# AdaLN block on one core: waits for scores placed per bank, x and statistics of the second half moved by one step, loads of rows and experts spread over steps

## What is computed

```python
mod = silu(c) @ wmod                       # six rows of 512 per batch: sa, ca, ga, sb, cb, gb
h = layernorm(x) * (1 + ca) + sa
q = rope(h @ Wq.T)                         # 32 heads of 128
k = low-rank c_kv = h @ Wdk.T, with 64 rotated columns per KV head from h @ Wkr.T   # 8 KV heads
v = c_kv @ Wupv.T
x = x + ga * (causal_softmax(q @ k.T / sqrt(128)) @ v) @ Wo.T
h = layernorm(x) * (1 + cb) + sb
p = softmax(h @ router.T + bias)           # 64 experts
w = p where it is among the 8 largest of its row, else 0
x = x + gb * (h * w.sum() + w @ expert_bias)
```

## Time and profile before

| | us |
|---|---|
| three timed executions | 1570.37, 1567.42, 1570.78; median 1570.37 |
| the profiled execution | 1571.39, of which the span of instructions 1570.1 |
| PE busy | 1507.3 (96% of the span) |
| DVE, POOL, ACT busy | 1174.6 (75%), 1031.4 (66%), 971.1 (62%) |
| share of PE in the chain of work that ended last | 89% |

### The profile page before, as it was taken

How to read it: one execution, slowest core, us unless ns; L and a number is a source line. 1 busy time by engine, 2 the same in 40 slices (tenths; PEclk the granted TensorE clock), 3 DMA queues, 4 the chain that set the end, 5 groups by cost and what they waited for, 6 DMA issues and landing times.

```text
span 1570.1 us, 24850 instructions
## 1 busy us (share of the span) xinstructions
PE 1507.3 (96%) x7502; PEld 1268.7 (81%) x7502; DVE 1174.6 (75%) x3437; ACT 971.1 (62%) x2301; POOL 1031.4 (66%) x778
## 2 busy tenths in 40 slices
PE   8979999999999999999999999998999999999978
PEld 5668888888888888888888888887887778787865
DVE  6856777777777777777777787775888888977746
ACT  3356766676676666676767677664656555565651
POOL 1776767676676677667667667665767777765612
PEclk9989999999999999999999999999999999999987
DMA  8547665566556656656556656658688776767631
GB/s 310 203 165 215 192 213 185 187 208 207 181 198 206 197 190 204 201 196 214 179 191 215 201 173 210 204 184 228 207 241 269 226 244 212 249 219 245 219 90 47
DMA packets 208245, 319.00 MB, mean 203 GB/s; under 512 B 37153, under 2 KB 125985, under 8 KB 208113
## 3 DMA queue, kind: packets, MB, share of 16 engines
q1 hardware_dynamic: 207792, 317.31, 62.9%
q10 hardware_dynamic: 320, 0.11, 0.0%
HBM read 177.71 MB, written 139.62 MB: 202 GB/s over the span
## 4 chain that ended last, share of the span: by engine, by line
PE 89%; DVE 3%; issue 3%; DMA 2%; ACT 1%; SPq 1%; POOL 1%; ACTq 0%; DVEq 0%
PE bank_s L465 22%; PE bank_o L563 21%; PE bank_pv L549 15%; PE bank_s L508 15%; PE bank_s L488 5%; PE bank_s L476 5%; PE bank_s L444 1%; PE bank_s L607 1%; PE bank_s L595 1%; DMA wmod<-in_wmod 1%; PE bank_o L412 1%; SPq L1639 1%; DMA PT_raw<-blocks 1%; DVE y L1037 1%; DMA blocks<-blocks 0%
## 5 line engine op out<-in xcount | busy, mean ns | idle before, releaser
L1460 POOL TENSOR_TENSOR PT_lo<-PT_raw,PT_hi 128x640 fp32r<-128x640 f32 x250 | 391.7, 1589 | 84.9 <-ACT PT_hi L841 84.8
L825 ACT ACTIVATE probs<-probs,row_inv 128x512 f32<-128x512 f32 x508 | 256.9, 554 | 169.7 <-DVE row_inv L1109 168.8
L1449 POOL TENSOR_TENSOR rot_c<-rot_c,rot_s 128x512 f32<-128x512 f32 x128 | 165.4, 1292 | 221.9 <-DVE rot_s L1070 221.9
L818 ACT ACTIVATE probs<-probs,row_min 128x512 f32<-128x512 f32 x508 | 278.4, 551 | 16.4 <-DVE row_min L1103 16.2
L1103 DVE CUSTOM_DVE_ANT_0 probs<-bank_s,mask 128x512 f32<-128x512 f32 x508 | 229.5, 487 | 0.9 <-issue 0.6
L1454 POOL TENSOR_TENSOR qT_lo<-rot_c,qT_hi 128x512 fp32r<-128x512 f32 x128 | 167.2, 1306 | 92.8 <-ACT qT_hi L800 92.8
L465 PE MATMUL bank_s<-hT_lo,wq_hi 128*128 128x512 f32 x500 | 205.2, 410 | 11.4 <-issue 9.3
L1126 DVE STREAM_TRANSPOSE blocks<-probs 128x384 f32<-128x384 f32 x500 | 201.9, 442 | 3.1 <-POOL hT_lo L1439 2.1
L465 PE MATMUL bank_s<-hT_hi,wq_hi 128*128 128x512 f32 x500 | 195.4, 391 | 0.0
L465 PE MATMUL bank_s<-hT_hi,wq_lo 128*128 128x512 f32 x500 | 195.3, 391 | 0.0
L563 PE MATMUL bank_o<-wo_lo,OT_hi 128*128 128x512 f32 x496 | 193.1, 389 | 1.4 <-DVE OT_lo L1134 1.4
(11 more groups left out here) (217 smaller groups left out, 3395.6 us busy)
## 6 DMA issues: line engine op xcount, KB each, us to landing
blocks<-blocks SPq DMA_DIRECT2D x125, 640.0 KB, 3.9
PT_raw<-blocks SPq DMA_DIRECT2D x500, 160.0 KB, 3.1
stage<-in_wq SPq DMA_DIRECT2D x32, 256.0 KB, 4.0
vblocks<-kv_raw SPq DMA_DIRECT2D x32, 256.0 KB, 4.3
kv_raw<-vblocks SPq DMA_DIRECT2D x128, 64.0 KB, 3.1
stage<-in_wo SPq DMA_DIRECT2D x32, 256.0 KB, 4.0
split_wq<-wq_hi SPq DMA_DIRECT2D x32, 256.0 KB, 3.9
split_wq<-wq_lo SPq DMA_DIRECT2D x32, 256.0 KB, 4.3
```

What stands on the lines that cost most here:

```text
L818: ins = act.activation(row(t, qt), row(t, qt), ACT.Exp, bias=row_min[m][:, qt:qt + 1], scale=-1.0, accum_out=row_sum[m][:, qt:qt + 1])
L825: ins = act.activation(row(t, qt), row(t, qt), ACT.Copy, scale=row_inv[t % 2][:, qt:qt + 1])
L1449: pool.tensor_tensor(rot_c[:], rot_c[:], rot_s[:], ALU.add).then_inc(pool_a, 1)
L1460: pool.tensor_tensor(PT[1][:, at], PT_raw[:, at], PT[0][:, at].bitcast(F32), ALU.subtract).then_inc(pool_t, 1)
```

## The change

1. In `scores` of a light step, the wait for the `weightT` copy stands ahead of query tile 2 (bank s2) and the wait for the `h2T` copy ahead of query tile 1 (bank s1). Query tile 3 (bank s3) waits for neither.
2. DVE's `ffn_x1` and `ffn_stats` of tile n move from the end of heavy step t to light step t+1, behind `mask_and_max`, ahead of the sums into y, `v_split_lo` and `q_rope`.
3. POOL's `ffn_stats` of tile n and `ffn_gate` of tile n+1 move from the end of heavy step t to the end of light step t+1.
4. SP loads the row tile n+1 at the end of the light step t+1 in place of the heavy step t. Rows of batch 0 come two each at steps 86 and 87, experts, router and bias at step 88, rows of batches 1 and 2 one at a time with row tiles 0 to 3 and 4 to 7.

```diff
--- before.py
+++ after.py
@@ -489,7 +489,7 @@
                                        start=(c == 0 and n == 0), stop=(c == CH - 1 and n == 2))
                 mm.then_inc(pe_v, 1)
 
-            def scores(t, tiles):
+            def scores(t, tiles, before=None):
                 if tiles[0] == QUERY_ORDER[0]:
                     pe.wait_ge(pool_q, t + 1)
                     if t % GROUP == 0:
@@ -504,6 +504,10 @@
                         pe.wait_ge(dve_kr, u + 2)
                     if qt == 2 and h == 0 and u > 0:
                         pe.wait_ge(dve_vt, u + 1)
+                    if qt == 2 and before is not None:
+                        tile_waits((wT_copy, before - 3), last=EARLY_TILES - 1)
+                    if qt == 1 and before is not None:
+                        tile_waits((h2T_copy, before - 1), last=EARLY_TILES - 1)
                     for n, (q, k) in enumerate(passes(qT[t % 2], kT)):
                         mm = pe.matmul(score_bank[qt], q[:, qt * P:(qt + 1) * P], k[:, 0:(qt + 1) * P],
                                        start=(n == 0), stop=(n == 2))
@@ -615,9 +619,7 @@
 
             def step(t):
                 u, h, n, before = t // GROUP, t % GROUP, ffn_tile(t), ffn_tile(t - 1)
-                if before is not None:
-                    tile_waits((wT_copy, before - 3), (h2T_copy, before - 1), last=EARLY_TILES - 1)
-                scores(t + 1, QUERY_ORDER)
+                scores(t + 1, QUERY_ORDER, before)
                 if t == 0:
                     pe.wait_ge(dve_h, BATCH * CH)
                 q_proj(t + 3)
@@ -1267,13 +1269,16 @@
                         dve.tensor_tensor(h2[m][:], h2[m][:], y[:, i, :], ALU.add).then_inc(dve_end, 1)
 
             def step(t):
-                u, h, n = t // GROUP, t % GROUP, ffn_tile(t)
+                u, h, n, before = t // GROUP, t % GROUP, ffn_tile(t), ffn_tile(t - 1)
                 mask_and_max(t + 1, 0)
                 if t >= 2 and not soon(t - 1):
                     o_split_lo(t - 2)
                 mask_and_max(t + 1, 1)
                 if n is not None:
                     ffn_norm(early(n - 1))
+                if before is not None:
+                    ffn_x1(early(before))
+                    ffn_stats(early(before))
                 if h == 2 and u > 0 and not soon(t - 2):
                     add_out(u - 1, range(2, QT))
                 if h == 0:
@@ -1297,9 +1302,6 @@
                 if soon(t):
                     o_split_lo(t - 1)
                     add_out(u - 1)
-                if n is not None:
-                    ffn_x1(early(n))
-                    ffn_stats(early(n))
 
             def last_step(t):
                 has1 = t + 1 < ALL
@@ -1521,8 +1523,9 @@
                     split_piece(CHUNKS[i], i % 2, chunk_event(g, i))
                 if n is not None:
                     ffn_out(early(n - 4))
-                    ffn_stats(early(n))
-                    ffn_gate(early(n + 1))
+                if before is not None:
+                    ffn_stats(early(before))
+                    ffn_gate(early(before + 1))
                 if t + 1 == FFN_FROM:
                     ffn_gate(0)
 
@@ -1673,25 +1676,27 @@
                     to = PT_raw[j * SUB:(j + 1) * SUB, :].rearrange("p (i x) -> p i x", i=SUBS)
                     sp.dma_start(to, rows[j]).then_inc(d_tr[t % 2], 16)
 
-            def load_rows(b):
-                if b < BATCH:
-                    sp.wait_ge(pe_qp, GROUP * last_unit(b) + GROUP)
-                    for n, tiles in enumerate((gate1, shift2, scale2, gate2)):
-                        sp.dma_start(tiles[b][:], mod_d[n, b:b + 1, :].broadcast_to([P, HID])).then_inc(d_rows[b], 16)
+            def load_rows(b, rows=range(4)):
+                sp.wait_ge(pe_qp, GROUP * last_unit(b) + GROUP)
+                for n in rows:
+                    to = (gate1, shift2, scale2, gate2)[n][b]
+                    sp.dma_start(to[:], mod_d[n, b:b + 1, :].broadcast_to([P, HID])).then_inc(d_rows[b], 16)
+
+            def load_experts():
+                sp.wait_ge(pe_qp, GROUP * last_unit(0) + GROUP)
+                sp.dma_start(experts[:], A["eb"]).then_inc(d_router, 16)
+                sp.dma_start(router[:], A["rw"]).then_inc(d_router, 16)
+                sp.dma_start(router_bias[:], A["rb"].broadcast_to([P, EXPERTS])).then_inc(d_router, 16)
 
             def ffn_load(i):
                 if 0 <= i < TILES:
                     if i == 0:
                         sp.wait_ge(pool_w, chunk_event(KV - 1, 3) + 1)
-                        sp.wait_ge(pe_qp, GROUP * last_unit(0) + GROUP)
-                        sp.dma_start(experts[:], A["eb"]).then_inc(d_router, 16)
-                        sp.dma_start(router[:], A["rw"]).then_inc(d_router, 16)
-                        sp.dma_start(router_bias[:], A["rb"].broadcast_to([P, EXPERTS])).then_inc(d_router, 16)
                     if i > 0:
                         sp.wait_ge(x1, i)
                     sp.dma_start(x_in[:], x_rows[i]).then_inc(d_xin, 16)
-                    if i % QT == 0 and i // QT + 1 < SHARED:
-                        load_rows(i // QT + 1)
+                    if i // QT + 1 < SHARED:
+                        load_rows(i // QT + 1, [i % QT])
 
             def store_out(i):
                 if 0 <= i < TILES:
@@ -1761,13 +1766,18 @@
                     load_values(u + 1)
                 if moved(t + 1):
                     store_blocks(t + 1)
-                n = ffn_tile(t)
+                n, before = ffn_tile(t), ffn_tile(t - 1)
                 if n is not None:
                     store_out(early(n - 4))
-                    if n < EARLY_TILES:
-                        ffn_load(n + 1)
+                if before is not None and before < EARLY_TILES:
+                    ffn_load(before + 1)
+                if t + 5 == FFN_FROM:
+                    load_rows(0, [0, 1])
+                if t + 4 == FFN_FROM:
+                    load_rows(0, [2, 3])
+                if t + 3 == FFN_FROM:
+                    load_experts()
                 if t + 1 == FFN_FROM:
-                    load_rows(0)
                     ffn_load(0)
             load_rows(BATCH - 1)
```

## The result

The change makes the kernel faster by 1.6%: 1545.69 us (median, 1541.4 to 1547.6) against 1570.57 us (1567.4 to 1571.5), a ratio of 0.9841 with the interval 0.9824 to 0.9859. The forecast was 1543, with a range of 1537 to 1554.

What follows compares the result with a forecast made beforehand. PE was taken as the bound, busy 96% of the span, so only its waits could move the end. Giving back 27.5 us takes 1571.4 to 1543.9, or 1543 for the median; range 1537 to 1554.

Steps and rivals of the forecast that it cites:

- The sum: Over the stretch under attention, 33.0 us of losses, of which the change gives back 8.6 + 9.8 + 9.1 = 27.5 us.
- Loss A: PE's hole of 6.9 us ahead of step 91's values product plus 1.7 at half clock: 8.6 us, all to go.
- POOL shows why: Step 91's hole: POOL's gate waited 11.31 us for batch 0 rows, with the probabilities' split PE needs queued behind it.
- Loss B: Scores' 14 stops for the copies of banks s2 and s1: 13.3 us with start-up, about 9.8 to be given back.
- "Nothing on top" for h = 2: Light steps with h = 2: DVE 0.4 us late, beside the remaining wait for bank s2, so no added loss.
- Loss C: q projection waiting until DVE has read bank s3 after the scores: 11.1 us, of which 2.0 was to stay.
- POOL's cover: Heavy steps: POOL's split ends 2.3 to 3.3 us later, still 1.8 us before the values product wants it.
- The spread loads: Earlier row and expert loads on SP: 0.43 to 0.71 us per issue, at most three a step, hidden.
- Rival 1: x always takes its long form, 1.7 us, making DVE late to the scores: gain 20, 1549 to 1551, chance 0.18.
- no work left beside x: Light steps: POOL has finished its split when DVE does x, so 2.0 us taken from a range of 0 to 5.4.
- Rival 4: PE's waits for bank s2 stay and DVE's lateness moves to heavy steps: 1556 to 1567, chance 0.07.
- Rivals 2 and 3: 2: PE's hole stays or recurs, 1552 us, chance 0.08; 3: late POOL stops PE once per tile, about 1575, chance 0.05.

Runs made afterwards that it cites:

- the best kernel: Changed kernel with weights transposed and copied first, output sums moved, ACT's copies before the q split in tiles 1 and 3, transposed values loaded first: 1537.25 us, ratio 0.9782.
- loads alone: Kernel before with only SP's loads of rows and experts spread over earlier steps, row tiles left in the heavy steps: 1560.86 us, ratio 0.9934.
- gate later: Kernel before with only POOL's first gate multiply moved from step 90 into step 91, behind the split; burst of 12 issues kept: 1572.52 us, ratio 1.0014.
- all three edits: Changed kernel with weights transposed and copied first, output sums moved to light steps, and ACT's copies before the q split in tiles 1 and 3: 1544.75 us, ratio 0.9841.
- sums later: Changed kernel with weights transposed and copied ahead of h2, and DVE's four output additions together in the light step with h = 2: 1545.92 us, ratio 0.9838.
- Values first: Changed kernel with SP loading the transposed values ahead of the transposed probabilities in steps with h = 3: 1541.80 us, ratio 0.9810.
- waits alone: Kernel before with only the scores' waits for the two copies placed per bank, ahead of query tiles 2 and 1: 1573.65 us, ratio 1.0016.
- waits and loads: Kernel before with waits placed per bank and loads spread, x and statistics left in the heavy step: 1564.44 us, ratio 0.9967.

## Why the prediction was right, point by point

**The sum.** Given back: 25.8 us between the profiled executions, 24.6 of it in the stretch, against 27.5 predicted. The account of what there was to gain held: A + B + C = 33.0 us, and the profiled execution of the best kernel is 1538.35, 33.0 below that of before (34.2 by ratio).

**Loss A: size right, cause half right.** 8.65 measured in the run with loads alone, 8.6 worked out, clock part included. The prediction's step "POOL shows why" named the gate's wait alone. The run with the gate later shows that it was the cause of the hole in step 91, but that the burst of 12 issues also delays the transposed probabilities behind it: with the gate moved on POOL alone, step 92 took 8.6 us more and step 93 3.4. How much of that is the burst's and how much the gate's new place is open. Spreading the issues left neither.

**Loss B: more left than worked out.** 3.5 us were to be left, 0.35 in each of ten places. The chain of step 108 shows 0.30; by step lengths the light steps with h = 0 are 0.31 over their floor of 12.10 and those with h = 2 are 0.48 over it, some 4.0 in ten places. "Nothing on top" for h = 2 was off by 0.17 a step; the chain has a second stop there, of 0.02, ahead of the q projection. What the sum did not have are the two stops in the table of after, 0.5 (step 94) and 0.7 (step 98); with them the light steps 94 to 116 stand 5.2 above their floor. ACT in after at both:

```profile
1103.26 0.63 ACT L802 ACTIVATE qT_hi<-rot_c 128x512 fp32r<-128x512 f32 x1 [2.72 <-POOL rot_c L1451]
1103.80 0.58 ACT L855 ACTIVATE stage<-bank_s 128x512 f32<-128x512 f32 x1
...
1149.57 0.63 ACT L802 ACTIVATE qT_hi<-rot_c 128x512 fp32r<-128x512 f32 x1 [2.98 <-POOL rot_c L1451]
```

The q split stands ahead of the copies in ACT's order and waits 2.7 to 3.0 us for POOL's rotation sum, which is late because POOL's split, with gate and root now ahead of it, is: POOL works without a wait from the gate at 1094.74 to the end of the rotation sum at 1103.22. The prediction followed POOL's delay to PE's values product and to SP, not to ACT. That ACT's order makes the stops is shown by the run with all three edits: sums later has them at 0.5 and 0.2, and with ACT taking the copies first both are gone. That POOL's delay is behind it is read from the rows; no run undoes it alone.

**Loss C: size near, reason wrong.** 2.0 us were to be left because DVE, with x in its longest light step, would come late to the next scores. Left are 2.7 in the table: 0.47 in step 97, 0.80 in 101, 0.75 in 118, 0.25 in 121, and 0.38 in 122, the one behind the last tile. In steps 97 and 101 DVE was not short of time: it had waited. DVE in step 108 of after, and POOL in step 109:

```profile
1276.24 1.25 DVE L1160 TENSOR_TENSOR y<-y,stage 128x512 f32<-128x512 f32 x1
...
1278.84 0.69 DVE L1092 TENSOR_TENSOR v_lo<-kv_raw,v_hi 128x512 fp32r<-128x512 f32 x1 [0.41 <-ACT v_hi L814]
```

```profile
1287.79 1.30 POOL L1484 TENSOR_TENSOR y<-y,gate 128x512 f32<-128x512 f32 x1
1289.05 3.29 POOL L1462 TENSOR_TENSOR PT_lo<-PT_raw,PT_hi 128x640 fp32r<-128x640 f32 x2
```

```profile
1278.17 0.63 ACT L814 ACTIVATE v_hi<-kv_raw 128x512 fp32r<-128x512 f32 x1 [2.72 <-DMA kv_raw<-vblocks]
```

The last line is ACT's, in step 108: it waits 2.72 us for the values and DVE behind it 0.41, which costs step 109 0.1 (12.00 for 11.90). In step 100 it is 3.63 and 1.78, and PE waits 0.80 in step 101. SP loads the values behind the probabilities, whose load waits for POOL's split. The prediction had that link ("SP's load ... moves as much, with the transposed values behind it") and gave it no price. This and the order on ACT, above, are the steps of its account that failed. Values first shows it: with only SP's order changed, the waits in steps 97, 101 and 121 go, 1.5 of the 2.7. The wait in step 118 is not x's: it stands at 0.75 in the run with the waits alone too, where x has not moved (0.13 before), and in after DVE's two additions into y, 1395.20 to 1396.45, stand right ahead of its read of those scores at 1396.38. Sums later takes these additions out of step 117, and the wait is gone. There the gain on the copies came back as a wait for DVE.

**POOL's cover held.** The split was to end 6.7 to 7.7 us after the scores' start, with 1.8 to spare. In after it ends at 1289.05 + 3.29 = 1292.34, 7.0 after the scores of that step begin in the chain at 1285.37, and no values product waits.

**The spread loads** were hidden, as said: the DMA share in step 98 fell from 0.98 to 0.82 (1149 to 1163 us in after), and steps 99 to 101 hold no wait of ACT for the transposed probabilities. The 0.67 worked out for such a step did not come: step 106, in which no row is loaded, has 0.79 too (1248.5 to 1262.5 us), where the prediction took 0.57 from before, so the share in such a window does not go by the rows alone.

**The rivals.** Rival 1 (which the prediction's text once calls the second), DVE as the next bound through x's long form, did not come, though the condition was met more often than not: in the twelve light steps x took 0.76 to 1.84, 1.44 in the median (0.91 before): long, 1.58 and more, in six, 1.25 to 1.30 in three and short in three. The rule of the Trainium skill that was cited (SBUF — State Buffer, section Who interferes with whom) makes the two exclude each other, and issue order decides who blocks. The trace agrees in all twelve: x always began while an instruction of POOL's split was running, and ended 0.54 or 0.55 us after that one's end. The shortest x, in step 98 of after:

```profile
1152.03 1.58 POOL L1462 TENSOR_TENSOR PT_lo<-PT_raw,PT_hi 128x640 fp32r<-128x640 f32 x1 [0.47 <-ACT PT_hi L843]
...
1153.39 0.76 DVE L1160 TENSOR_TENSOR y<-y,stage 128x512 f32<-128x512 f32 x1
```

The split's instruction ends at 1153.61 and x at 1154.15; in step 108, whose x is shown above, they end at 1276.94 and 1277.49. So x met POOL's split every time, as the prediction had it under rival 1 and not as its sum had it ("no work left beside x"), but its length is what is left of POOL's instruction and not always the long figure. It cost little: in steps with h = 0 DVE had time to spare, and in four of the six it waited for `v_hi` behind x, 0.24 to 1.78 us; the waits of steps 97 and 101 stand behind two of the three shortest x, 0.81 and 0.78. In those with h = 2 the step is some 0.17 longer. Rival 4, waits that move without shrinking, is exactly what the waits per bank do without x. Its chance was given to the whole change; it belonged to the part. Rivals 2 and 3 did not appear.

**Where the sum was lucky.** It adds three losses and takes each part's gain from its own loss. The table of parts shows that B and C are not two losses but two stops in one row on PE, ahead of the same read by DVE: taking away the first alone gives it to the second (9.3 becomes 16.7 or 17.0), and joined they can cost the clock. The other way round it works: x takes the second stop away without the first. The sum is right only for the whole, where both go, and there too its terms lean on each other: in the order loads, x, waits the stretch of the profiled executions gave 10.0, 8.5 and 6.1 us against 8.6, 9.1 and 9.8. The term that was furthest off is loss B's.

## What to carry to other kernels

Where an in-order engine stops twice within one step, look for what ends the second stop before pricing the first: if it is work on another engine that starts at its own time, the first gain comes back as the second wait, and the edit on the first stop pays only together with one on the second (here the second paid alone, 7.2 us). Follow a delayed instruction to everyone who waits for it, through each queue (here POOL's split to ACT's q split, and to SP's load and ACT's values), and price every link, also the one that seems covered. The burst of 12 loads delayed all that stood behind it on the queue, and moving its first victim only found the next; spreading it cost nothing that could be seen.

## What the runs showed of the hardware that was not expected

- One pause of PE could be dearer than two of nearly the same sum. In step 98 of before, pauses of 0.7 and 1.0 us, 2.1 us apart, left the granted clock at 1.00; the one pause of 1.87 us in waits alone was followed by about 3.4 us at 0.50 (1.2 GHz), which cost 1.8 us more. With waits and loads a pause of 1.59 at 1259.0 us was followed by a q projection of 4.58, and one of 1.61 at 1207.1 by one of 2.96: the length of the pause alone does not tell which it will be, and the runs do not show what does.
- The four issues of one load of transposed probabilities took SP 1.80 us in a quiet place (values first) and 4.69 behind the burst of 12 (gate later). The issue itself was stretched, and not only the landing.
- PE lost 0.3 us where the table of waits shows none (step 108 of after): 0.03 of waiting in the middle of a run of twelve matmuls and 0.27 in their time.
- An addition on DVE (x) that began during an instruction of POOL's split ended 0.54 or 0.55 us after it, in twelve cases of twelve; without POOL beside it it takes 0.67.
